# A graph network on one core: a block that ends without waiting for its stores, and a last stage in one pass

## The reference, cut to what matters

```python
# layer 0: messages into a GRU
msg = h[src] @ W_msg.T + b_msg + edge_embed[edge_type]
x = layernorm(x + gru(segment_sum(msg, dst), h))
# layer 1: gated attention, mean over the edges
proj = x @ fc_weight.T
e = sum(leaky_relu(proj[src] + proj[dst], 0.2) * attn)
w = sigmoid(e * sigmoid(sum(proj[src] * proj[dst])))
neigh = segment_sum(x[src] * w, dst) / max(degree, 1)
x = layernorm(x + (1 + eps) * x + neigh)
```

## Time and profile before

| | |
|---|---|
| median of 3 runs | 3324.41 us (3315.03 to 3326.8) |
| the profiled execution, its own time | 3325.84 us |
| its span in the profile | 3324.0 us |
| busy: VectorE | 2487.7 us |
| busy: GpSimd | 2221.1 us |
| busy: TensorE matmul | 2133.7 us |
| busy: ScalarE | 1562.8 us |
| mean granted TensorE clock | 0.775 |

### The profile page before, as it was taken

One profiled execution on the slowest core, in us unless ns is written; L12 is line 12 of the kernel. 1 busy time (PEld: TensorE's weight loads), 2 busy tenths in 40 slices (PEclk: granted clock), 3 DMA queues, 4 the chain that ended last, 5 costly groups with the idle time before them and its releaser, 6 DMA issues. The chain is left out here.

```text
span 3324.0 us, 64226 instructions
## 1 busy us (share of the span) xinstructions
PE 2133.7 (64%) x13619; PEld 1702.8 (51%) x13619; DVE 2487.7 (75%) x12615; ACT 1562.8 (47%) x3370; POOL 2221.1 (67%) x2275
## 2 busy tenths in 40 slices
PE   1398988999899845555555555655555555555553
PEld 1266666666674444444445554544554545444442
DVE  6566666666654578888887887888888888888888
ACT  2255544455553345445454454454454454545541
POOL 2467777777730037777777777777777777777772
PEclk9999999999999877677676667666666666766665
DMA  7222222222220085555555555555555555555562
GB/s 138 79 68 76 74 74 74 76 76 75 77 79 1 23 235 156 169 163 157 169 160 161 168 158 165 164 157 167 165 156 169 163 159 168 159 164 164 158 168 66
DMA packets 364818, 431.96 MB, mean 130 GB/s; under 512 B 178859, under 2 KB 247845, under 8 KB 364788
## 3 DMA queue, kind: packets, MB, share of 16 engines
q0 software_dynamic: 107760, 274.39, 29.0%
q1 hardware_dynamic: 254815, 156.62, 17.7%
q10 hardware_dynamic: 2212, 0.60, 0.1%
HBM read 407.68 MB, written 23.70 MB: 130 GB/s over the span
## 5 line engine op out<-in xcount | busy, mean ns | idle before, releaser
L1385 POOL DMA_INDIRECT got<-rows,idx x1624 | 1548.1, 953 | 536.0 <-issue 510.1
L1551 PE MATMUL sum_ps<-whot,got 128*128 128x128 f32 x3264 | 680.4, 377 | 663.2 <-DVE whot L1397 590.7
L1551 PEld LDWEIGHTS sum_ps<-whot,got 128*128 128x128 f32 x3264 | 585.4, 269 | 750.6 <-DVE whot L1397 658.5
L727 POOL DMA_INDIRECT got<-x_rows,idx x616 | 625.0, 1015 | 196.6 <-issue 187.4
L1544 PE MATMUL er_ps<-win,hot_t 128*128 128x128 bf16 x4932 | 524.5, 284 | 254.7 <-ACT hot_t L1495 230.5
L870 ACT CAST work<-c_ps 128x318 bf16<-128x318 f32 x1008 | 420.0, 428 | 482.4 <-PE c_ps L943 473.8
L1453 DVE CUSTOM_DVE_ANT_0 pr_s<-got,er_ps 128x128 f32<-128x128 f32 x1624 | 370.2, 284 | 363.8 <-DMA got<-rows,idx 357.9
L1544 PEld LDWEIGHTS er_ps<-win,hot_t 128*128 128x128 bf16 x4932 | 464.9, 133 | 297.0 <-ACT hot_t L1495 260.0
L894 PE MATMUL span_ps<-x_parts,work 128*126 128x393 bf16 x2544 | 583.9, 339 | 0.0
L1397 DVE TENSOR_SCALAR whot<-iota_f,dl,w_s 128x128 f32<-128x128 f32 x1632 | 459.1, 359 | 0.3 <-ACT w_s L1500 0.3
L1525 ACT ACTIVATE r_s<-er_ps 128x512 f32<-128x512 f32 x406 | 242.4, 597 | 381.3 <-DVE er_ps L1465 379.1
(11 more groups left out here) (238 smaller groups left out, 1823.5 us busy)
## 6 DMA issues: line engine op xcount, KB each, us to landing
work<-dst_row SPq DMA_DIRECT2D x413, 256.0 KB, 3.7
got<-rows,idx POOLq DMA_INDIRECT x1624
win<-parts SPq DMA_DIRECT2D x118, 96.0 KB
got<-x_rows,idx POOLq DMA_INDIRECT x616
idx<-src_rows SPq DMA_DIRECT2D x413, 2.0 KB
parts<-split SPq DMA_DIRECT2D x13, 384.0 KB, 3.3
x_rows<-x_parts SPq DMA_DIRECT2D x1, 4641.0 KB
rows<-nodes SPq DMA_DIRECT2D x13, 256.0 KB, 3.5
```

What stands on the lines that cost most here:

```text
L727: pool.indirect_dma_start(got[:, c, i, 0:3 * D], None, x_rows, bass.IndirectOffsetOnAxis(ap=idx[:, c, i:i + 1], axis=0)).then_inc(gathered ...
L1385: pool.indirect_dma_start(got[:, c, i, :], None, rows, bass.IndirectOffsetOnAxis(ap=idx1[:, c, i:i + 1], axis=0)).then_inc(gathered[c], 16)
L1551: mm = pe.matmul(sum_ps[:, 0:P], got[:, c, i, D:2 * D], whot[:, c, i, :], start=(c == 0 and i == 0), stop=(c == NS - 1 and i == STEP - 1))
```

## The change

SP's three final waits leave the preparing block and stand at the head of SP's program in the counting block. The buffers that stores still read then are moved or kept: `first_k`, `first_ki` and `column_ki` live on into the counting block; `dst_t` and `type_h` now lie in a part of `nodes` that the counting block does not clear, and `src_i` in a part of `sums`. GpSimd therefore clears `counts` before `sums`, and waits for `left_out` and `dst_out` between them.

The last stage drops GpSimd and the split at tile 40. ScalarE scales `nodes` by `c_x` in the edge stage, between its six chunks ahead and its loop. In the last stage TensorE runs four quads deep; VectorE mixes each tile in one instruction from PSUM, takes the statistics, and prepares scale and offset of the quad before; ScalarE takes the root of a quad and normalises the quad two before. VectorE normalises only the last quad. SP stores by fours in order.

```diff
-                    sp.wait_ge(left_out, 16 * (2 + (br > 0)))
-                    sp.wait_ge(dst_out, 48)
-                    sp.wait_ge(tables_out, 48)
...
+                    sp.wait_ge(left_out, 16 * (2 + (CT % ROWS > 0)))
+                    sp.wait_ge(dst_out, 48)
+                    sp.wait_ge(tables_out, 48)
                     body, bodies, tmp = (sp.alloc_register(...) ...)
...
                     pool.memset(nodes[:, ft:NTL, :], 0.0).then_inc(nodes_set, 1)
+                    pool.memset(counts[:, 0:NPAD], 0.0).then_inc(zeroed0, 1)
+                    pool.wait_ge(left_out, 16 * (2 + (CT % ROWS > 0)))
+                    pool.wait_ge(dst_out, 48)
                     pool.memset(sums[:, 0:NPAD], 0.0).then_inc(zeroed0, 1)
-                    pool.memset(counts[:, 0:NPAD], 0.0).then_inc(zeroed0, 1)
...
+                    for q in range(NQ):
+                        t = slice(q * QUAD, (q + 1) * QUAD)
+                        act.activation(nodes[:, t, :], nodes[:, t, :], ACT.Copy, scale=c_x[:]).then_inc(scaled, 1)
                     with every_body(act) as k:
...
                 def _(act):
+                    def root(q):
+                        act.wait_ge(agreed, QUAD * (q + 1))
+                        act.activation(rstd[:, q * QUAD:(q + 1) * QUAD], moments[:, q * QUAD:(q + 1) * QUAD, 1],
+                                       ACT.Sqrt, bias=low_bound[:]).then_inc(rooted, 1)
+                    def normalise(q):
+                        act.wait_ge(shifted, q + 1)
+                        for t in range(q * QUAD, (q + 1) * QUAD):
+                            act.activation(nodes[:, t, :], nodes[:, t, :], ACT.Identity, scale=rstd[:, t:t + 1],
+                                           bias=offset_s[:, t:t + 1]).then_inc(finished_act, 1)
+                    act.wait_ge(bound_set, 1)
+                    for q in range(NQ):
+                        root(q)
+                        if q >= 2:
+                            normalise(q - 2)
+                    normalise(LAST - 1)
...
                 def _(dve):
+                    def scale_of(q):
+                        t = slice(q * QUAD, (q + 1) * QUAD)
+                        dve.wait_ge(rooted, q + 1)
+                        dve.reciprocal(rstd[:, t], rstd[:, t]).then_inc(inverse, 1)
+                        dve.wait_ge(inverse, q + 1)
+                        dve.scalar_tensor_tensor(out=offset_s[:, t], in0=moments[:, t, 0], scalar=-1.0,
+                                                 in1=rstd[:, t], op0=ALU.mult, op1=ALU.mult).then_inc(shifted, 1)
+                    dve.wait_ge(scaled, NQ)
                     for q in range(NQ):
                         dve.wait_ge(m_turned, q + 1)
+                        for i in range(QUAD):
+                            t = q * QUAD + i
+                            dve.scalar_tensor_tensor(out=nodes[:, t, :], in0=m_ps[:, q % 4, i, :],
+                                                     scalar=rdeg[:, t:t + 1], in1=nodes[:, t, :],
+                                                     op0=ALU.mult, op1=ALU.add).then_inc(mixed, 1)
+                        for i in range(QUAD):
+                            dve.wait_ge(mixed, q * QUAD + i + 1)
+                            dve.bn_stats(stats[:, i, :], nodes[:, q * QUAD + i, :]).then_inc(stated, 1)
+                        if q >= 1:
+                            scale_of(q - 1)
+                        for i in range(QUAD):
+                            dve.wait_ge(stated, q * QUAD + i + 1)
+                            dve.bn_aggr(moments[:, q * QUAD + i, :], stats[:, i, :]).then_inc(agreed, 1)
+                    scale_of(LAST)
+                    dve.wait_ge(shifted, NQ)
+                    for t in range(LAST * QUAD, NTL):
+                        dve.tensor_scalar(nodes[:, t, :], nodes[:, t, :], rstd[:, t:t + 1], offset_s[:, t:t + 1],
+                                          ALU.mult, ALU.add).then_inc(finished, 1)
```

More of the change, by code:

```diff
@@ L134, in graph_layers @@
         chunk_begun = sem("chunk_begun")
+        scaled = sem("scaled")
         x_out = sem("x_out")
+        left_out = sem("left_out")
+        dst_out = sem("dst_out")
+        tables_out = sem("tables_out")
         @contextmanager
@@ L174, in graph_layers @@
             dst_i = sb("dst_i", [P, TILES], I32, ph)
-            dst_t = sb("dst_t", [P, TILES], F32, ph)
+            dst_t = flat_nodes[:, 3 * CTX:3 * CTX + TILES]
             type_i = sb("type_i", [P, TILES], I32, ph)
-            src_i = sb("src_i", [P, TILES], I32, ph)
-            type_h = sb("type_h", [P, TILES], F16, ph)
+            src_i = sums[:, 4 * CTX:4 * CTX + TILES].bitcast(I32)
+            type_h = flat_nodes[:, 3 * CTX + TILES:3 * CTX + TILES + -(-TILES // 2)].bitcast(F16)[:, 0:TILES]
             iota_i = sb("iota_i", [P, P], I32, ph)
@@ L1577, in graph_layers @@
         with ExitStack() as ph:
-            mean_s = sb("mean_s", [NODES, QUAD, D], F32, ph)
-            m_ps = psum("m_ps", [NODES, 2, QUAD, D], F32, ph)
+            m_ps = psum("m_ps", [NODES, 4, QUAD, D], F32, ph)
+            low_bound = sb("low_bound", [NODES, 1], F32, ph)
+            offset_s = sb("offset_s", [NODES, NTL], F32, ph)
+            bound_set = sem("bound_set")
             m_turned = sem("m_turned")
-            steps = sem("steps")
-            spread = sem("spread1")
+            mixed = sem("mixed")
+            stated = sem("stated")
+            agreed = sem("agreed")
+            rooted = sem("rooted")
+            inverse = sem("inverse")
+            shifted = sem("shifted")
             finished = sem("finished")
+            finished_act = sem("finished_act")
             stored = sem("stored")
[L1585 to L1592, removed]
+            LAST = NQ - 1
             with nc.Block() as block:
@@ L1630, in _ @@
-                    dve.wait_ge(steps, S * NQ + 1)
-                    dve.tensor_scalar(rstd[:], moments[:, :, 1], LN_EPS, None, ALU.add).then_inc(spread, 1)
-                    dve.wait_ge(spread, 2)
-                    dve.reciprocal(rstd[:], rstd[:]).then_inc(spread, 1)
-                    dve.wait_ge(spread, 3)
-                    dve.sem_inc(spread, 1)
-                    normalise(dve, range(0, HERE), finished)
-                @block.gpsimd
-                def _(pool):
-                    pool.wait_ge(spread, 4)
-                    normalise(pool, range(HERE, NTL), finished_pool)
+                            dve.wait_ge(mixed, q * QUAD + i + 1)
@@ L1645, in _, with wait_for @@
                     n = 0
-                    starts = sorted(range(0, ft, 4), key=lambda t: t - (HERE if t >= HERE else 0))
-                    for at in starts:
+                    def wait_for(tiles):
+                        sp.wait_ge(finished_act, min(tiles, LAST * QUAD))
+                        if tiles > LAST * QUAD:
+                            sp.wait_ge(finished, tiles - LAST * QUAD)
+                    for at in range(0, ft, 4):
                         m = min(4, ft - at)
-                        if at >= HERE:
-                            sp.wait_ge(finished_pool, at - HERE + m)
-                        else:
-                            sp.wait_ge(finished, at + m)
+                        wait_for(at + m)
                         sp.dma_start(out[at * NODES:(at + m) * NODES, :].rearrange("(t p) f -> p t f", p=NODES),
```

39 lines of the change are left out of this document (10 added, 29 removed).

## The result

The changed kernel takes 3305.05 us (median of six runs, 3302.64 to 3307.66) where the kernel before takes 3322.98 beside it (3315.03 to 3326.8): ratio 0.9946, 95% interval [0.9932, 0.996], 17.9 us less by the medians. The prediction was 3307.6 us, 16.8 us less. The profiled execution has 3307.66 us over a span of 3305.8, against 3325.84 over 3324.0 before: 18.2 us less.

What follows compares the result with a forecast made beforehand. Gathers on GpSimd were taken to bound the edge stage, and VectorE's quads, then the tail behind them, the last stage. Terms -3.2 + 2.8 - 16.4 = -16.8 us off the 3324.41 us median gave 3307.6 us; range 3300 to 3316 us.

Steps and rivals of the forecast that it cites:

- The waits, -3.2: End of preparing: SP's wait for its last store leaves the path, so counting starts 3.2 us earlier.
- The rival that the end of a block waits for stores: End of preparing: the block itself waits for open stores, so preparing gives nothing; 3310.8 us, chance 0.07.
- The rival of a vanished gap: End of preparing: VectorE starts counting at 88, not held for SP; 3276.8 us, chance 0.02.
- The scaling, +2.8: Edge stage: 13 ScalarE scalings take 8.0 us, of which 2.8 us come through, paid once.
- the slack, 5.2 us said: Edge stage: GpSimd wanted a sum at 1245.28 that was there at about 1240.1, 5.2 us to spare.
- The copies hold back more than one gather: Edge stage: listed sign that the prediction is wrong; it expected one gap of about 2.8 us near 1242.
- The rival that pays all 8.0 us: Edge stage: the scaling is paid in full, as GpSimd is not the limit from its start; 3312.8 us, chance 0.08.
- The quad, 2.45: Last stage: VectorE's time per quad falls from 2.76 to 2.45 us, with four short mixes replacing two long instructions.
- 18.4 for 16.4: Last stage as a whole, quads and tail: forecast to give -16.4 us.
- the end, 7.6 for 8.0: Last stage's tail: the span ends about 8 us behind the last aggregate.
- The rival of a quad of 2.8 us: Last stage: quads do not get shorter, as VectorE's 5 more instructions eat the gain; 3312.0 us, chance 0.11.

Runs made afterwards that it cites:

- e2: Only the new last stage and ScalarE's 13 scalings, with SP's waits where the kernel before has them: ratio 0.9951 to the kernel before.
- e4: The changed kernel with a second, neutral round of 13 scalings (scale 1) behind the first: ratio 0.997 to the kernel before.
- e3: The changed kernel with the 13 scalings by `c_x` left out altogether: ratio 0.9923 to the kernel before.
- e5: The changed kernel with 8 of the 13 scalings ahead of ScalarE's loop and 5 behind it: ratio 0.9939 to the kernel before.
- e9: The changed kernel repeated without an edit in a later comparison: 3318.3 us, ratio 0.9965 to the kernel before.
- e6: The changed kernel with the `x_rows` store issued in the counting block, behind SP's three waits: ratio 0.9948 to the kernel before.
- e10: The changed kernel without the 13 scalings, taken once more in a later comparison: ratio 0.9947 to the kernel before.
- e11: The changed kernel with the `x_rows` store in halves, SP issuing the first once ready, ScalarE's queue the second: 3300.62 us, ratio 0.9905 to the kernel before.
- e12: The changed kernel with both the halved `x_rows` store and the scalings split 8 before and 5 behind ScalarE's loop: 3297.59 us, ratio 0.9898 to the kernel before.
- e1: Only SP's moved waits and buffers, with the last stage of the kernel before and no scalings: ratio 0.999 to the kernel before.
- e8: The changed kernel with a sigmoid, from another table, in place of ScalarE's last normalisation: 3331.13 us in a single execution.

## Why the prediction was right

**The waits, -3.2.** Right. The first memset came 2.6 us earlier, though preparing itself ran 0.85 us later in this execution (the `x_rows` issue starts at 76.60 against 75.75): against that issue it is 3.5. The forecast was 118.7 for the memset and 130.8 for the first gather; they came at 119.31 and 131.60. The rival that the end of a block waits for stores is out: the block ended with SP's wait of 2.8 us still ahead. The rival of a vanished gap is out too: VectorE's first instruction of the counting block stands at 119.88, with GpSimd's.

**The scaling, +2.8.** Right in mechanism; 3.6 was measured. The 13 instructions take 8.05 us (8.0 said), the delay arrives nearly whole at VectorE (7.9), and the slack takes up the rest. The gather that sets the total is the one named, wanted at 1245.28 before: its sum comes at the half of the row of 16 matmuls, now at 1242.49. The mis-sized term is the slack, 5.2 us said and 7.9 - 3.6 = 4.3 measured: the gather starts 2.8 us behind that row's start, not the 2.0 that half of its length gives. What the prediction put at nothing is the 0.8 us from the end of a sum to the start of the gather that it releases (1236.07 + 2.08 = 1238.15 against 1238.96); half of 3.80 and 0.8 are 2.7. How long the sum itself takes goes with TensorE's granted clock: over that row it was 0.50 before and 0.52 after (the lower of its two levels, 1.2 GHz, nearly throughout). In e2 it was 1.00 there (2.4 GHz), the sum took 1.16 us, and the gather came 1.97 us behind its start:

```profile
1246.07 1.16 PE L1555 MATMUL sum_ps<-whot,got 128*128 128x128 f32 x8 [1.25 <-DVE sums L1424]
...
1248.04 0.94 POOL L1386 DMA_INDIRECT got<-rows,idx  x1 [0.79 <-PE sum_ps L1555]
```

The two late gathers of e2 cost (2.56 - 0.3) + (0.79 - 0.3) = 2.8 us, the forecast's number, but by a faster sum and the 0.8 us. The other profiles, at 0.50 to 0.54 there, have 3.3 to 3.7 us. So which of the two it is goes with the clock of the execution.

That the gather four before it (1240.28 before) is late as well was missed: it had 7.9 - 2.2 = 5.7 us of slack, and its 2.2 us are the first part of the same 3.6, not an addition. "The copies hold back more than one gather" was on the prediction's list of what would show it wrong; two were held back, but the delay is still paid once. e4 fits: 16.0 - 4.3 = 11.7, and 11.6 measured. The rival that pays all 8.0 us is against the traces; the timing can't exclude it.

**The quad, 2.45.** 2.35 was measured: 12 x 0.10 = 1.2 us of the 2.0 by which the last stage came out better (18.4 for 16.4). The four mixes start 0.25 us apart, as said, where one lasts 335 ns. The 0.10 are 0.04 in the reciprocal and offset (0.27 for 0.31), 0.03 in the aggregates (0.29 for 0.32) and the little that was added for more starts. The rest is in the start, 0.4, and in the end, 7.6 for 8.0. The start goes with the clock of that execution and not with the change: the first mix is 0.7 us behind the first transpose at a granted clock of 1.00; it was 1.1 before, at 0.50, and the new last stage has 1.1 to 1.2 too where it begins at 0.50. Of the profiles with this last stage, the five with 1.00 there (the change, e2, e3, e5, e9) take 38.7 to 38.8 us, the five with 0.50 (e4, e6, e10, e11, e12) 39.1 to 39.3. The rival of a quad of 2.8 us is out. ScalarE's tile of 128x128 takes 479 ns, and eight in 3.17 us start 0.385 apart (0.40 said). The Trainium skill, "ScalarE: Activation LUTs", section "Table sets: the hidden batching unit", has identity in every set; the trace agrees, with one load of 1.28 us in the stage. That load came late, at 3270.08, behind the wait for the first moments, and was hidden.

**What the sum left out.** The terms as measured are -2.6 + 3.6 - 18.4 = -17.4 of the profile's 18.2 us. The table has -4.8 us in counting, for which the prediction had nothing. The group of all gathers of that stage says what most of it is: they are busy 621.0 us, 1008 ns each, where the kernel before has 625.0 us and 1015 ns. Before:

```profile
L727 POOL DMA_INDIRECT got<-x_rows,idx x616 | 625.0, 1015 | 196.6 <-issue 187.4 <-DMA idx<-src_rows 9.2
```

In the changed kernel:

```profile
L731 POOL DMA_INDIRECT got<-x_rows,idx x616 | 621.0, 1008 | 195.8 <-issue 187.7 <-DMA idx<-src_rows 8.1
```

In e9, the same kernel as after:

```profile
L731 POOL DMA_INDIRECT got<-x_rows,idx x616 | 625.8, 1016 | 196.1 <-issue 187.9 <-DMA idx<-src_rows 8.2
```

There the stage takes 886.1 us, against 885.8 before. e1 has 621.0 us of gathers and 879.7, e3 627.7 and 888.8. So the stage goes with the length of the gathers in that execution, not with the edit. The middle stages move between 200.1 and 206.8 us over the profiles in no order that an edit gives. The granted clock has a part in it: the two shortest (200.1, e1 and e8) have 0.91, the others 0.87 to 0.89; but 202.2 and 206.3 stand at the same 0.88, so the rest stays open.

**How near it was.** By the first comparison the miss is 1.1 us (16.8 for 17.9), by e9's 5.1 us (11.7, interval 7.7 to 16.0). So small a miss is in part luck: the terms missed by +0.6, +0.8 and -2.0, and cancel to -0.6. The first time, 3305.05, is within the range; e9's own median of 3318.3 stands beside a kernel before that is 5.5 us slower in that comparison than the 3324.4 from which the forecast starts, and its 11.7 us less than 3324.4 would be 3312.7, within the range as well. e9's profile has 14.0 us less than before: -3.0 preparing, +3.6 late gathers, -18.3 last stage, and +3.7 for the rest, 3.0 of it gathers of edges that are busy 1551.1 us instead of 1548.1. Its terms are all there. That the timed repeats differ for the same reason is likely, but was only seen in the profiled executions.

## What to carry to other kernels

Price work that is put into an engine with idle time by the slack at the first thing that comes too late on the engine that sets the pace, not by its length: 8 us cost 3.6, and the next 8 cost 8.0. When a stage waits for a queue, look at whether the queue waits or issues, and at what is behind it on that queue: taking away the wait gave 3 us, moving the issue gave none, and splitting it over two queues, with its first half issued as soon as that was ready, gave 16. The largest gain here is neither: work that stood behind the last quad (20.1 us) now runs beside the quads, and 7.6 are left. Several short instructions can beat fewer wide ones when they do the work in one pass instead of two (1.01 against 1.51 us a quad); whether one wide pass would beat four short ones wasn't measured.

## What the runs showed of the hardware

- An issue stands in its queue behind a large store: behind the 6188 rows of `x_rows` SP's next issue stands for 38.4 us, at 117 GB/s with the DMA engines at 0.42. With half of the rows on each of two queues the same window has 150 GB/s at 0.47, and the `x_rows` issues are through in 32.3 us, not 38.8. The Trainium skill, "DMA: Bandwidth & Descriptors", section "Issuing engines are not separate DMA queues", says that initiating on several engines saves only the sequencer's time, usually small. Here a second queue also raised what the engines moved. Whether the queue or some of the engines limit the store is not shown, as 0.42 is a mean over all 16.
- A short VectorE instruction (0.3 us elsewhere) stands for 10.46 us beside GpSimd's memsets and ends as the last one does (131.13, 130.99). The Trainium skill, "SBUF — State Buffer", section "Who interferes with whom", has an exclusive lock on a port pair for this; the trace agrees that VectorE stands still until a memset ends. With the memset of `counts` first, VectorE got no turn between the two long memsets; with that of `sums` first, as before and in e2, two instructions ended between them (4.96 us, to 128.09). Why the order matters is open.
- The gathers of the counting stage are busy 620.1 to 627.7 us over the fourteen profiles, those of the edge stage 1546.5 to 1552.9, in numbers and shapes that never change: up to 7.6 and 6.4 us between two executions, as much as the smaller terms of this change.
- A table load has no further cost visible beside its 1.28 us: in e8 each of the two in a round starts at once behind the instruction before it, and the next instruction at once behind it. The Trainium skill, "ScalarE: Activation LUTs", section "What ACT_TABLE_LOAD costs", gives 2.66 us with the drain; here the round of 4.58 us has room for 1.28 twice only.
